# An expert's upward product copied to SBUF before its tanh, and a pass's first weights fetched at its beginning

## The reference, cut to what matters

```python
# layer 3's expert part; layers 0 and 1 have the same gate, without biases
h = einsum('md,ndh->nmh', x, Wl1) + bl1          # the upward product: halves a and b
a, b = h[..., :H], h[..., H:]
y = einsum('nmh,nhd->nmd', silu(a) * b, Wl2) + bl2
out = einsum('mn,nmd->md', ew, y)                # ew: weights of the two chosen experts
```

## Time and profile before

| what | value |
|---|---|
| median of 3 runs | 4476.97 us (4469.98 to 4478.3) |
| the profiled execution, as a run | 4474.15 us |
| its span in the trace | 4471.6 us |
| PE busy | 86% of the span |
| ACT busy | 87% |
| DVE busy | 65% |
| POOL busy | 18% |
| mean granted TensorE clock | 0.968 of full speed |

### The profile page before, as it was taken

One profiled execution on the slowest core, in us unless ns is written; L12 is line 12 of the kernel. 1 busy time (PEld: TensorE's weight loads), 2 busy tenths in 40 slices (PEclk: granted clock), 3 DMA queues, 4 the chain that ended last, 5 costly groups with the idle time before them and its releaser, 6 DMA issues.

```text
span 4471.6 us, 69696 instructions
## 1 busy us (share of the span) xinstructions
PE 3844.3 (86%) x26742; PEld 881.7 (20%) x26742; DVE 2892.4 (65%) x5746; ACT 3897.2 (87%) x4328; POOL 820.2 (18%) x705
## 2 busy tenths in 40 slices
PE   8888888988889888898979998888888888888886
PEld 2121112211122211222212221111111111112112
DVE  6878898788877788877603332110785588877823
ACT  4689998899988899889899899989987889888994
POOL 3110001510035200252512111111001110044002
PEclk7699999999999999999999999999999999999998
DMA  6220001100021110111102221110011000010001
GB/s 157 56 63 25 12 12 33 35 12 12 17 60 31 46 25 17 33 36 34 33 19 63 64 71 27 39 40 17 14 31 27 27 12 12 14 43 24 5 1 50
DMA packets 124482, 151.31 MB, mean 34 GB/s; under 512 B 29272, under 2 KB 76384, under 8 KB 124080
## 3 DMA queue, kind: packets, MB, share of 16 engines
q1 hardware_dynamic: 123424, 146.41, 12.2%
q10 hardware_dynamic: 720, 0.40, 0.0%
HBM read 123.21 MB, written 23.51 MB: 33 GB/s over the span
## 4 chain that ended last, share of the span: by engine, by line
PE 49%; ACT 27%; DVE 13%; issue 6%; DMA 1%; SPq 0%; POOL 0%; ACTq 0%; POOLq 0%; DVEq 0%
PE av L884 20%; ACT prob L1045 17%; DVE mpart L1156 10%; PE scores L874 8%; PE side L906 5%; ACT above L1053 5%; PE scores L984 4%; PE side L1002 4%; PE side L984 2%; DVE above L1160 2%; PE scores L897 1%; ACT ag L1096 1%; ACT tx L1087 1%; PE side L874 1%; PE scores L1026 1%
## 5 line engine op out<-in xcount | busy, mean ns | idle before, releaser
L1045 ACT ACTIVATE prob<-scores 128x1024 f32<-128x1024 f32 x2998 | 2948.2, 1036 | 249.1 <-PE scores L874 221.8
L1156 DVE TENSOR_REDUCE mpart<-side 128x1 f32<-128x512 f32 (+1 forms) x3456 | 2132.8, 657 | 625.6 <-PE side L906 613.1
L884 PE MATMUL av<-prob,VA 128*9 128x512 f32 x6528 | 867.5, 604 | 40.5 <-ACT prob L1045 37.5
L884 PE MATMUL av<-prob,VB 128*9 128x512 f32 x6528 | 864.8, 602 | 18.7 <-ACT prob L1045 17.9
L874 PE MATMUL scores<-QP,KA 32*128 32x512 f16 x2996 | 562.0, 390 | 145.8 <-ACT above L1053 81.7
L874 PE MATMUL scores<-QP,KB 32*128 32x512 f16 x3000 | 554.3, 385 | 144.3 <-ACT above L1053 71.1
L906 PE MATMUL side<-KA,QP 32*128 32x512 f16 (+1 forms) x2112 | 618.1, 390 | 41.9 <-DVE mpart L1156 34.2
L906 PE MATMUL side<-KB,QP 32*128 32x512 f16 (+1 forms) x2112 | 578.1, 379 | 35.8 <-DVE mpart L1156 32.9
L1160 DVE CUSTOM_DVE_ANT_0 above<-side,above 128x512 f32<-128x512 f32 x768 | 516.3, 686 | 79.3 <-PE side L906 65.2
L1053 ACT ACTIVATE above<-scores 128x1024 f32<-128x1024 f32 x384 | 394.1, 1026 | 113.1 <-DVE mpart L1160 59.0
L1045 ACT ACTIVATE prob<-side 128x1024 f32<-128x1024 f32 x266 | 288.5, 1085 | 24.3 <-PE scores L874 23.8
(11 more groups left out here) (197 smaller groups left out, 2713.0 us busy)
## 6 DMA issues: line engine op xcount, KB each, us to landing
cwb<-weights SPq DMA_DIRECT2D x80, 256.0 KB, 3.9
KA<-kstacks SPq DMA_DIRECT2D x384, 48.0 KB
KB<-kstacks SPq DMA_DIRECT2D x384, 48.0 KB
Fin<-in_Fin SPq DMA_DIRECT2D x64, 256.0 KB, 2.8
kstacks<-hi SPq DMA_DIRECT2D x100, 128.0 KB, 2.4
ctxc<-in_ctxT SPq DMA_DIRECT2D x36, 256.0 KB, 3.0
hT<-in_mask SPq DMA_DIRECT2D x16, 400.2 KB, 3.5
kstacks<-lo SPq DMA_DIRECT2D x50, 128.0 KB, 2.6
```

The source lines that it names most:

```text
L884: last = pe.matmul(AV[ROWS * h:ROWS * h + VC, :], V[l % 2][:, kt, g * HG + h, :], prob[:, (e + h // 2) % RING, (h % 2) * QB:(h % 2) * QB + ...
L1045: act.activation(prob[:, e % RING, :], pair.rearrange("p a b -> p (a b)"), ACT.Exp if softmax(l) else ACT.Sigmoid, scale=SCALE).then_inc(s ...
L1156: dve.tensor_reduce(part, bank, AX.X, ALU.max).then_inc(sem["red"], 1)
```

## The change

ACT's two steps of a (k, j) change places: `ac` comes first and waits for `up`, and `tanh` comes second, waits for `ac` and reads the copy in SBUF in place of the PSUM bank. In layer 3 the bias is then in the copy already, so `tanh` has no bias operand any more; the halved bias `b1h` and the DVE instruction that made it are gone, and `ac` of layer 3 waits for the load of the biases itself. The `wexp` steps of a pass's first three experts move from behind `cwput` to the beginning of the pass.

```diff
--- before.py
+++ after.py
@@ -203,7 +203,7 @@
     if s.what == "ksplit":
         return 3 if SPLITS[s.key[1]][1] else 2
     return {"routea": 2 if l == 3 else 1, "routef": 2, "routeg": 2, "routeh": 2, "routej": 2, "routek": 2, "routel": 2, "routec": 5,
-            "routed": 3 if l == 0 else 1, "bqs": 2, "b1s": 2, "mflag": 2}.get(s.what, 1)
+            "routed": 3 if l == 0 else 1, "bqs": 2, "b1s": 1, "mflag": 2}.get(s.what, 1)
 
 
 class Order:
@@ -319,7 +319,8 @@
 
     l, b = unit(u)
     f = FFN[l]
-    out = [(6, Step("PE", "logit", (u, lp)))]
+    out = [(0, Step("SP", "wexp", (u, lp, k))) for k in range(W_RING)]
+    out += [(6, Step("PE", "logit", (u, lp)))]
     out += [(3 if what == "routea" else 2, Step("DVE", what, (u, lp))) for what in ("routea", "routeb", "routee", "routef", "routeg", "routeh")]
     out += [(2, Step("ACT", "rexp", (u, lp)))]
     out += [(4 if what == "routej" else 2, Step("DVE", what, (u, lp))) for what in ("routej", "routek", "routel")]
@@ -327,8 +328,6 @@
         out += [(2, Step("DVE", "routec", (u, lp))), (6, Step("PE", "count", (u, lp)))]
     out += [(2, Step("DVE", "routed", (u, lp))), (4, Step("PE", "cwT", (u, lp))), (1, Step("ACT", "cwTc", (u, lp))),
             (2, Step("SP", "cwput", (u, lp)))]
-    for k in range(W_RING):
-        out.append((0, Step("SP", "wexp", (u, lp, k))))
     out.append((0, Step("SP", "cwget", (u, lp, 0))))
     if f["gated"] and l != 3:
         out.append((0, Step("POOL", "xk", (u, lp, 0))))
@@ -358,8 +357,8 @@
             if j == 0 and k + 1 < E:
                 out.append((0, Step("POOL", "xk", (u, lp, k + 1))))
             return
+        out.append((0, Step("ACT", "ac", (u, lp, k, j))))
         out.append((0, Step("ACT", "tanh", (u, lp, k, j))))
-        out.append((0, Step("ACT", "ac", (u, lp, k, j))))
         out.append((1, Step("PE", "up", (u, lp, k, n + j))))
         if by_dve(u, lp):
             out.append((2, Step("DVE", "gatea", (u, lp, k, j))))
@@ -734,7 +733,6 @@
         rbias = sb("rbias", [P, 2, E])
         normw = sb("normw", [P, D])
         b1 = sb("b1", [P, E, 4])
-        b1h = sb("b1h", [P, E, 2])
         b2 = sb("b2", [E, D])
         b2d = sb("b2d", [E, D])
         hT = sb("hT", [P, H_RING, QB])
@@ -1078,14 +1076,10 @@
                     u, lp, k, j = s.key
                     l = unit(u)[0]
                     fs, ch = FFN[l]["fs"], 2 * k + j
-                    own.wait_ge(*(o.sem("ac", u, lp, k, j) if u == 3 else o.sem("up", u, lp, k, j)))
-                    if l == 3:
-                        own.wait_ge(*o.sem("b1s", 3))
+                    own.wait_ge(*o.sem("ac", u, lp, k, j))
                     if ch >= 2:
                         own.wait_ge(*o.sem("gatea" if by_dve(u, lp) else "gateb", u, lp, k - 1, j))
-                    a = ag[0:fs, ch % 2, 0, :] if u == 3 else bank_of(o, "up", u, lp, k, j)[0:fs, :]
-                    act.activation(tb[0:fs, ch % 2, :], a, ACT.Tanh, scale=0.5,
-                                   bias=b1h[:, k, j:j + 1] if l == 3 else 0.0).then_inc(sem["bgA"], 1)
+                    act.activation(tb[0:fs, ch % 2, :], ag[0:fs, ch % 2, 0, :], ACT.Tanh, scale=0.5).then_inc(sem["bgA"], 1)
                 elif s.what == "ac":
                     u, lp, k, j = s.key
                     l = unit(u)[0]
@@ -1093,6 +1087,8 @@
                     own.wait_ge(*o.sem("up", u, lp, k, j))
                     if ch >= 2:
                         own.wait_ge(*o.sem("gateb", u, lp, k - 1, j))
+                    if l == 3:
+                        own.wait_ge(*o.sem("wffn", 3))
                     act.activation(ag[0:fs, ch % 2, 0, :], bank_of(o, "up", u, lp, k, j)[0:fs, :], ACT.Identity if l == 3 else ACT.Copy,
                                    bias=b1[:, k, j:j + 1] if l == 3 else 0.0).then_inc(sem["bgA"], 1)
                 elif s.what == "gc":
@@ -1389,7 +1385,6 @@
                         dve.tensor_scalar(bq[l % 2][:, j, :], bqr[l % 2][:], factor, None, ALU.mult).then_inc(sem["bgV"], 1)
                 elif s.what == "b1s":
                     own.wait_ge(*o.sem("wffn", 3))
-                    dve.tensor_scalar(b1h[:], b1[:, :, 0:2], 0.5, None, ALU.mult).then_inc(sem["bgV"], 1)
                     dve.tensor_scalar(b2d[:], b2[:], 2.0, None, ALU.mult).then_inc(sem["bgV"], 1)
```

## The result

The changed kernel takes 4481.58 us (median of 22 runs, 4474.73 to 4487.04) where the kernel before takes 4473.83 us (22 runs beside it, 4467.0 to 4485.49). The ratio is 1.0014, with a 95% interval of 1.0008 to 1.0020: slower by 3.6 to 8.9 us, within the 0.2% that I had called no change. The forecast was 4485 and +8.3 us, range 4470 to 4495. The profiled execution took 4480.93 us with a span of 4475.6 us.

A forecast was written before the change was run, and what follows sets the result against it. No engine bounds alone; beside attention the tanh and ac pairs lie on the chain. Reordering +14.6 us (12.2 + 1.6 + 0.8) and earlier fetch -6.3 (4.7 + 1.6) give +8.3 us, 4485 us, range 4470 to 4495.

The forecast's parts named there:

- What bounds: No engine bounds alone; beside attention nearly every tanh and ac pair is on the chain, so added ACT time reaches the end.
- Part 1, (a) and (b): Pairs beside attention: tanh from SBUF, waiting for the copy, costs +0.19 us in 64 pairs (12.2), +0.10 in unit 6 (1.6).
- Part 1, (c): Pairs beside attention: ac gives the PSUM bank back 0.49 us earlier, taken as a gain of 0.
- Part 2: Unit 7, nothing beside it: the reordered tanh and ac cost +0.09 us, 9 times, 0.8 us.
- Part 3: First weights fetched at the pass's beginning: -4.7 us in unit 7, -1.6 us in unit 3, 0 elsewhere.
- The sum: Whole kernel: +14.6 us for the reordered steps, -6.3 us for the earlier weight fetch, +8.3 us together, 4485 us.
- Release: Rival: the earlier bank release lets PE start dif and scores sooner, giving 4472 or 4446 us; chance 0.08.
- A dear wait: Rival: ACT empties and restarts between copy and tanh, gap some 0.25 us, not 0.04, giving 4504 us; chance 0.12.
- No loss of overlap: Rival: each of 64 pairs loses 0.09 us, not 0.19, the others nothing, giving 4476.5 us; chance 0.04.
- Absorbed: Rival: ACT's idle time takes up its added time and only the fetch gain is left, giving 4471 us; chance 0.06.
- fetch not earlier: Rival: something else holds SP's queue at the pass's beginning, so the weights gain nothing, giving 4491 us; chance 0.04.

The follow-up runs named there:

- the swap with the late release: Kernel before with ac ahead of tanh, tanh reading SBUF, first weights fetched as before, bank given back at tanh except in unit 3: 4490.59 us, ratio 1.0038.
- the fetch alone: Kernel before with only the first wexp weight loads moved to the beginning of the pass, tanh and ac as before: 4470.41 us against 4476.37, ratio 0.9987.
- the swap alone: Changed kernel with the first weights fetched behind cwput as before; against the kernel before: 4492.69 us against 4476.37, ratio 1.0039.
- the later tanh: Changed kernel with tanh moved behind the second up of its pair; against the kernel before: 4459.46 us against 4476.09, ratio 0.9962.
- the order alone: Kernel before with ac ahead of tanh, both reading PSUM, no wait between them, bank given back behind tanh: ratio 0.9995.
- order and wait: Kernel before with ac ahead of tanh, both reading PSUM, bank given back behind tanh, and tanh waiting for ac: ratio 1.0031.

## Why the prediction was right

**What bounds.** Right. The pairs lie on the chain, and what ACT is slowed down by arrives in the time: 0.19 us longer from the copy to the exp, 0.17 us in the phase.

**Part 1, (a) and (b).** The gap between copy and tanh was taken as 0.04 us from a row of DVE and is 0.03; the tanh's 0.54 us held. The pair is 1.16 us as forecast. The sum for 64 pairs was 12.2 us and is 64 x 0.17 = 10.9 us, because the exps behind are 0.03 us shorter. Unit 6: forecast 1.6, measured 0.65 us for 8 pairs, 1.3 in all if the other 8 cost as much.

**Part 1, (c).** Release worth 0: shown by the swap with the late release. That the waits of weight loads overstate a wait was the right reading.

**Part 2.** Forecast +0.8 us in unit 7, measured +0.4. Before, `gatea` started 0.10 us behind the end of `ac`; after, it starts 0.04 us behind the end of tanh (4436.48), and an expert took 5.88 us (`down` at 4432.25 and 4438.13) instead of 5.86 (4433.70 and 4439.56):

```profile
4435.85 0.63 ACT L1082 ACTIVATE tx<-ag 128x512 f32<-128x512 f32 x1
4436.52 0.69 DVE L1311 SCALAR_TENSOR_TENSOR ag<-tx,ag 128x512 f32<-128x512 f32 x1 [0.96 <-ACT tx L1082]
```

**Part 3.** The mechanism was right in both units and both sizes were off, to different sides. Unit 7: forecast -4.7, measured -3.74 with the fetch alone. The first tanh does come 5.1 us sooner behind `cwT` (2.76 against 7.90 us), but the clock does not. It had fallen to 1.2 GHz (0.50) at 4387.2 us, after PE had been busy for 0.33 us in the stretch from 4384 to 4386, and stayed there through the routing. Before, it came back 3.3 us after `up` had begun (4414.5); with the fetch alone it took 5.0 us (4413.2), so more of the first products ran at half speed. Windows of before and of the fetch alone:

```profile
4411.02:4413.02 2.00, 1.87 (x2) 0.83 (x3) 0.00 (x0) 0.00 (x0) 0.00 (x0) 0.50 0.81 228
4413.02:4415.02 2.00, 2.00 (x4) 0.85 (x3) 0.39 (x1) 1.27 (x2) 0.00 (x0) 0.63 0.79 282
```

```profile
4409.01:4411.01 2.00, 2.00 (x4) 0.97 (x3) 0.00 (x0) 0.90 (x2) 0.00 (x0) 0.50 0.05 8
4411.01:4413.01 2.00, 2.00 (x3) 0.72 (x3) 1.41 (x2) 0.36 (x1) 0.00 (x0) 0.50 0.55 184
4413.01:4415.01 2.00, 2.00 (x6) 0.81 (x5) 0.24 (x2) 1.27 (x2) 1.27 (x1) 0.96 0.21 78
```

1.7 us more at half clock is 0.85 us of full clock, which is most of what is missing. In the two profiles of the changed kernel the clock came back 3.6 and 5.2 us after `up`, and from `cwT` to the output it was -4.29 and -3.86; less the swap's 0.4 the fetch is worth 4.7 and 4.3 there. So the forecast of 4.7 was met in the one profile in which the clock came back early. No run changes the clock alone: this is read from four profiles.

Unit 3: forecast -1.6, the two waits that PE had. Phases 16 and 18 average -2.35 and -1.17 us in the five profiles with the early fetch and -0.66 and -0.13 in the seven without: -2.7 us. The term counted only PE's own idle time ahead of `up`; the chain before went through SP's six issues and a `cwb` that took 6 us to land, and ACT stood idle for 1.40 us behind it as well. These phases hold half clock stretches, so 2.7 is rough. Where they hold equally much half clock (6.8 us in phase 16 in five profiles with the early fetch and five without; in phase 18 3.4 us in four and three), the differences are -1.3 and -0.8: -2.1 us.

**The sum.** By phases 10.9 + 1.3 for the swap beside attention, -2.7 for unit 3, and -4.1 for unit 7 with both edits (mean of the two profiles): +5.4 us. The runs say +7.75, 3.6 to 8.9 (+6.6 by their means). Of that some 2.6 us lie outside the span, where no term of the forecast was, which leaves 4 to 5 us inside it. So the closeness of 8.3 to 7.75 is in part luck: inside the span the forecast was about 3 us too high, 2 of them in the swap (14.6 against 12.6 by phases), and the time outside the span made up for it. The parts are right in kind and near in size: +14.6 lies in a measured +11 to +23 and -6.3 in -1.8 to -10.3.

The time outside the span came with the swap: on average 4.1 to 5.0 us in the swap alone, with the late release and with the later tanh, 2.1 to 2.3 in the fetch alone, the order alone and order and wait, as before. No run tells whether the tanh's source, the missing `b1h` or the new wait for the biases brings it.

**The rivals.** Release: fallen. A dear wait: fallen, 0.03 us and not 0.25. No loss of overlap: fallen, 0.14 us for the wait. As the prediction applied it, the Trainium skill's rule of a bubble that is not pipelined between instructions (Advanced Engine Details and Errata, The Read-Write Bubble) gave the wrong cost: the starts are 0.49 us apart without the wait and 0.62 with it. The rows don't speak against a bubble as such. An exp of 1024 columns starts 0.92 us before the next (two last 1.94 us, one 1.02), 0.43 more than the 0.49 of an instruction of 512, so by an estimate from these rows some 0.06 us between starts doesn't grow with the width. Absorbed and fetch not earlier: fallen.

**What stays open.** Phase 0 was 3.9 to 4.6 us longer in both profiles of the changed kernel than in both of before. It goes with the time that PE spends at half clock in it (summed over windows of 2 us): 126 us in both profiles of before, 130 in the three that were longer by 0.7 to 1.4 us, and 133 to 143 in the seven longer by 3.9 to 7.0. For a given kernel it moves too, 137 us of half clock and +4.28 against 130 and +1.23 for the later tanh. The order alone, with +5.2 and +5.9 in phase 0, is not slower than before in 11 runs (0.9995), and the 4 to 5 us by which the spans of the changed kernel are longer are used up by the other phases. That speaks for chance of the executions that were profiled; why the half clock lasts longer in one of them, and whether it or the delay comes first, no run shows. The cause of the time outside the span is open too.

## What to carry to other kernels

Ask of a reordering on a busy engine which instruction the next engine waits for: here it was the exp behind the pair, so two steps in either order cost the same, a wait between them cost 0.14 us, and moving one of them out from ahead of the exp gained 0.18. A copy that frees a PSUM bank pays through the freedom to do the rest later, and not by the bank itself, if no product waits for the bank; waits on the row of weight loads don't show that one does. Compare phases at fixed marks of the trace, with a control, before a few microseconds are given to a cause, and compare the spans with the times: part of a difference can lie outside the span.

## What the runs showed of the hardware that was not expected

- A DMA of 16 KB from SBUF to DRAM had landed at most 1.46 us after its issue (2417.32 to 2418.78), sooner than the estimate that stands beside the sum of the prediction. `cwb`, 256 KB, reached POOL 3.55 us after its own issue, where right behind six loads of weights it had taken 6.19 (2405.61 to 2411.80).
- A stretch of half clock at the same place of one kernel lasted 3.4 us in one execution and 10.2 in the next, and the phase was 2.1 us longer (phase 28).
- The exps behind an SBUF tanh were shorter, 1.91 us for two in place of 1.94; I have no cause for it.
